# A selective scan on four engines: one activation table set, a bank of its own for the in-projection, GpSimd's states moved, and VectorE's two products as one instruction

## The reference

```
xc = conv1d(x, conv_w) + conv_b                     # 4 taps, one channel at a time
x_dbl = xc @ xproj_w.T                              # 64 dt columns, 16 B, 16 C
dt = clip(x_dbl[:64] @ dtproj_w.T + dtproj_b, 1e-5, 1.0)
u = clip(xc, -10, 10)
delta = softplus(dt + dtproj_b)
A = -exp(A_log)
h[n](t) = exp(delta(t) * A[n]) * h[n](t-1) + delta(t) * u(t) * B[n](t)      # n = 0..15
y(t) = sum_n h[n](t) * C[n](t) + u(t) * D
```

## Time and profile before

| | us |
|---|---|
| median of 3 runs | 9635.69 (9633.86 to 9641.92) |
| the profiled execution | 9635.57 |
| its span | 9633.7 |
| busy: PE, DVE, ACT, POOL | 7457.1, 7666.2, 5757.0, 7469.2 |
| TensorE's mean granted clock | 0.869 of full speed |

### The profile page before, as it was taken

The page is one execution under the profiler, slowest core; times in us unless marked ns, Lnnn a source line. Parts: engine busy times, 40 slices in busy tenths (PEclk is TensorE's granted clock), DMA queues, the critical chain, the costliest instruction groups (busy, mean ns, idle before and its releaser), DMA issues. The chain is left out here.

```text
span 9633.7 us, 148574 instructions
## 1 busy us (share of the span) xinstructions
PE 7457.1 (77%) x28632; PEld 4225.4 (44%) x28632; DVE 7666.2 (80%) x8365; ACT 5757.0 (60%) x12996; POOL 7469.2 (78%) x3329
## 2 busy tenths in 40 slices
PE   7477778787878787865587777787777778659999
PEld 3243444444444444444244444444444444434444
DVE  7924989898989898999298989898989898964444
ACT  3634767676767676766376767676767676640000
POOL 2115999999999999999299999999999999961110
PEclk9689998888888888876788989898989898869999
DMA  2263121212121212110223232323232322133442
GB/s 80 60 184 113 59 100 58 100 57 100 57 100 58 99 58 100 57 62 20 96 67 108 68 108 67 108 64 108 66 106 70 106 68 101 46 126 132 139 140 82
DMA packets 638321, 842.03 MB, mean 87 GB/s; under 512 B 210320, under 2 KB 357776, under 8 KB 620688
## 3 DMA queue, kind: packets, MB, share of 16 engines
q1 hardware_dynamic: 638096, 839.98, 26.9%
HBM read 586.47 MB, written 253.28 MB: 87 GB/s over the span
## 5 line engine op out<-in xcount | busy, mean ns | idle before, releaser
L1102 POOL TENSOR_TENSOR fwd_w<-fwd_du,fwd_bcast_b 128x2048 f32<-128x2048 f32 x504 | 2275.4, 4527 | 19.4 <-DMA fwd_bcast_b<-bc 3.5
L1102 POOL TENSOR_TENSOR bwd_w<-bwd_du,bwd_bcast_b 128x2048 f32<-128x2048 f32 x504 | 2275.8, 4528 | 15.9
L1174 DVE TENSOR_TENSOR_SCAN bwd_h<-bwd_da,bwd_state,bwd_w 128x512 f32<-128x512 f32 x1536 | 1879.0, 1269 | 2.0 <-POOL bwd_w L1102 2.0
L1174 DVE TENSOR_TENSOR_SCAN fwd_h<-fwd_da,fwd_state,fwd_w 128x512 f32<-128x512 f32 x1536 | 1878.9, 1269 | 2.0 <-POOL fwd_w L1102 2.0
L909 PE MATMUL bwd_yT<-all_ident,bwd_hc 128*128 128x128 f32 x6144 | 1058.8, 306 | 899.4 <-DVE bwd_hc L1186 895.8
L909 PE MATMUL fwd_yT<-all_ident,fwd_hc 128*128 128x128 f32 x6144 | 1036.9, 301 | 827.5 <-DVE fwd_hc L1186 823.7
L1023 ACT ACTIVATE fwd_da<-fwd_delta,fwd_aneg 128x512 f32<-128x512 f32 x2048 | 1399.5, 686 | 148.2 <-DVE fwd_h L1174 146.6
L1023 ACT ACTIVATE bwd_da<-bwd_delta,bwd_aneg 128x512 f32<-128x512 f32 x2048 | 1399.2, 686 | 148.0 <-DVE bwd_h L1174 146.5
L909 PEld LDWEIGHTS bwd_yT<-all_ident,bwd_hc 128*128 128x128 f32 x6144 | 785.1, 155 | 1455.9 <-DVE bwd_hc L1186 1181.8
L909 PEld LDWEIGHTS fwd_yT<-all_ident,fwd_hc 128*128 128x128 f32 x6144 | 773.1, 153 | 1394.8 <-DVE fwd_hc L1186 1096.1
L1186 DVE TENSOR_TENSOR fwd_hc<-fwd_h,fwd_bcast_c 128x512 f32<-128x512 f32 x1536 | 1005.2, 681 | 369.0 <-ACT fwd_state L992 338.7
(11 more groups left out here) (181 smaller groups left out, 11538.7 us busy)
## 6 DMA issues: line engine op xcount, KB each, us to landing
bwd_win<-winx SPq DMA_DIRECT2D x128, 512.0 KB, 3.3
fwd_win<-winz SPq DMA_DIRECT2D x128, 512.0 KB, 3.5
yT<-bwd_y_out SPq DMA_DIRECT2D x129, 256.0 KB, 2.7
yT<-fwd_y_out SPq DMA_DIRECT2D x129, 256.0 KB, 3.2
fwd_x<-x_pad SPq DMA_DIRECT2D x128, 257.5 KB, 2.7
n_xin<-x SPq DMA_DIRECT2D x64, 512.0 KB, 4.2
x_pad<-bwd_x SPq DMA_DIRECT2D x128, 256.0 KB, 2.9
xc<-bwd_xc_out SPq DMA_DIRECT2D x128, 256.0 KB, 2.0
```

Source lines behind the costliest of these rows:

```text
L1102: nc.gpsimd.tensor_tensor(w[:, g], du[:, s].unsqueeze(1).to_broadcast([P, G, T]), bcast_b[:, g * G:(g + 1) * G], ALU.mult).then_inc(S["w_d ...
L1174: nc.vector.tensor_tensor_scan(flip(h_slot(n)), flip(da[:, p % 3]), flip(w[:, n // G, n % G]), state_at(j, s, end, n), ALU.mult, ALU.add). ...
```

## The change

Four things change, all inside `stage_scan`:

1. `preload_act_table_set("natural_log_exp_and_others")` stands once per direction, in the prologue. The built program then has no table load in the loops.
2. da has two banks in place of three; `misc` is split in two, `dt_ps` (dt and the convolution) and `in_ps` (the in-projection). ScalarE saves h[n-2] ahead of exp n, and waits for scan n-2.
3. GpSimd's states are 2, 5, 8 and 11, so that VectorE's are 0, 1, 3, 4, 6, 7, 9, 10 and 12 to 15: each pair is followed by a scan of one of GpSimd's states, but for the last two pairs. The steps at which the other pieces stand move with it. On GpSimd the clip of dt is written as min, then max.
4. VectorE multiplies both states of a pair in one instruction of 128x1024 (`weigh_two`), over both banks of h and two neighbouring slots of hc.

```diff
-PN = [0, 3, 6, 9]
+PN = [2, 5, 8, 11]
...
-        da = sc.ps("da", [P, 3, T])
+        da = sc.ps("da", [P, 2, T])
...
-        misc = sc.ps("misc", [P, T])
+        dt_ps, in_ps = sc.ps("dt_ps", [P, T]), sc.ps("in_ps", [P, T])
...
-        LATE = 5
-        IN, IN2, CONV, PROJ, SKIP = 2, 7, 8, 13, 12
-        POOL_AT = [5, 9, 10, 14]
+        LATE = 3
+        IN_AT, IN2_AT, CONV, PROJ, SKIP = (0, 2), (8, 11), 5, 11, 11
+        POOL_AT = [5, 8, 11, 14]
...
                     for n in range(NS):
-                        act.wait_ge(S["scan_done"], m * 32 + (s * 16 + n - 2 + SCR))
+                        act.wait_ge(S["scan_done"], m * 32 + (s * 16 + n - 1 + SCR))
+                        save(j, s, end, n)
...
-                        nc.scalar.activation(da[:, (s * NS + n) % 3], delta[:, s], ACT.Exp,
+                        nc.scalar.activation(da[:, n % 2], delta[:, s], ACT.Exp,
                                              scale=aneg[:, s, n:n + 1]).then_inc(S["exp_done"], 1)
...
+                nc.scalar.preload_act_table_set("natural_log_exp_and_others")
...
-                nc.gpsimd.tensor_scalar(v[:], dt[:], 1e-5, 1.0, ALU.max, ALU.min).then_inc(S["v_done"], 1)
+                nc.gpsimd.tensor_scalar(v[:], dt[:], 1.0, 1e-5, ALU.min, ALU.max).then_inc(S["v_done"], 1)
...
                     weigh_c(ub, 0, k)
                     weigh_b(s, ub, 3, k)
-                    weigh_c(ub, 1, k)
-                    weigh_c(ub, 2, k)
                     if late:
                         clip_v(ub + 1)
-                        weigh_c(ub, 3, k)
+                    weigh_c(ub, 1, k)
+                    if late or not nxt:
+                        weigh_c(ub, 2, k)
                     if nxt:
                         scan_input(1 - s, ub + 1, p_loads)
+                        if not late:
+                            weigh_c(ub, 2, k)
                         weigh_b(1 - s, ub + 1, 0, k2, single=late)
-                    if not late:
-                        weigh_c(ub, 3, k)
+                    weigh_c(ub, 3, k)
...
+                    def weigh_two(n):
+                        p, i = s * NS + n + 1, s * NV + VN.index(n) + 1
+                        for g in sorted({n // G, (n + 1) // G}):
+                            dve.wait_ge(c_loaded[g], k * LOAD + LOAD)
+                        dve.wait_ge(S["scan_done"], m * 32 + p + 1 + SCR)
+                        dve.wait_ge(S["hc_used"], m * (2 * NV) + i + 1)
+                        if a or not end or s == 0 or n + 1 < NS - 2:
+                            dve.wait_ge(S["h_saved"], m * (2 * NS) + (p + 3))
+                        nc.vector.tensor_tensor(hc[:, (i - 1) % NOUT:(i - 1) % NOUT + 2], h[:],
+                                                bcast_c[:, n:n + 2], ALU.mult).then_inc(S["hc_done"], 2)
 
                     for n in range(NS):
                         scan(n)
-                        if n in VN and VN.index(n) % 2:
-                            weigh(VN[VN.index(n) - 1])
-                            weigh(n)
+                        if n in PN:
+                            weigh_two(n - 2)
+                        if n in (NS - 3, NS - 1):
+                            weigh_two(n - 1)
```

More of the change, by code:

```diff
@@ L856, in pair @@
                     for n in range(NS):
[L857 to L865, removed]
-                            dt_matmul(1 - s, (m + s) * (NPL * LOAD) + NPL * LOAD)
-                            if late:
-                                open_projection()
[L869 to L886, removed]
-                            projection(1, ma)
-                            close_projection()
-                        if n == SKIP:
-                            pe.wait_ge(S["ud_done"], ub + 3)
-                            for tb in range(TB):
-                                nc.tensor.matmul(yT[:, tb], ud[:, s, tb * P:(tb + 1) * P], ident[:],
-                                                 is_transpose=True, start=False, stop=False)
                         if n in POOL_AT:
@@ L1028, in pair @@
+                        if with_in and not (end and s == 1) and n == 7:
+                            in_copy(s, ma, m)
+                        if nxt and n == ln_at:
+                            ln_step(b_p1)
+                        if n == ud_at:
                             nc.scalar.activation(ud[:, s], u[:, s], ACT.Copy,
                                                  scale=skip[:, s]).then_inc(S["ud_done"], 1)
-                        if nxt and n == read_at:
-                            act.wait_ge(p_in[1 - s], (m + s) * (NPL * LOAD) + NPL * LOAD)
-                            dt_read(1 - s, m * 2 + s + 2)
@@ L1033, in pair @@
-                        if nxt and n in ln_steps:
-                            softplus_tail(1 - s, m * 2 + s + 2, ln_steps.index(n))
-                        if a and n == 5 and not late:
-                            diagonal(s, ma)
-                        if a and end and s == 0 and n == 12:
+                        if a and not late and n == 10:
+                            xc_copy(s, ma)
+                        if a and end and s == 0 and n == 13:
                             diagonal(1, ma)
-                        if with_in and not (end and s == 1) and n == 9:
-                            in_copy(s, ma, m)
@@ L1041, in pair @@
-                        if with_in and end and s == 0 and n == 14:
+                        if with_in and end and s == 0 and n == 15:
                             in_copy(1, ma, m)
-                        if a and not end and n == 14:
-                            xc_copy(s, ma)
-                        if late and n == 2:
-                            xc_copy(0, ma)
+                        if late and n == 4:
+                            xc_copy(1, ma)
                         if late and n == 5:
-                            xc_copy(1, ma)
@@ L1049, in pair @@
-                        if late and n == 7:
                             proj_copy(k + 1)
@@ L1056, in between @@
                 dt_read(0, 1)
-                for step in range(3):
-                    softplus_tail(0, 1, step)
-                nc.scalar.preload_act_table_set("exp_and_others")
+                abs_step(0, 1)
+                exp_step(0, 1)
+                ln_step(1)
+                relu_step(0, 1)
             def prologue():
```

121 lines of the change are left out of this document (79 added, 42 removed).

## The result

| | us |
|---|---|
| before, median of 4 runs | 9634.78 (9631.48 to 9641.92) |
| after, median of 4 runs | 9911.96 (9908.77 to 9922.27) |
| ratio | 1.0289, 95% interval [1.0271, 1.0306] |
| predicted | 9239 (9145 to 9430) |

The account below looks back on a forecast made before the run. VectorE (27.34 us a block) and GpSimd (27.17) nearly level, taken as 27.5 with coupling, against 29.05 before: gain 1.55 x 256 = 397 us, 9635.6 - 397 = 9239 us, range 9145 to 9430.

Parts of the forecast that it names:

- TensorE at nothing: TensorE's in-projection gets its own bank, starts at the block's first step, has until 10.2 us: cost nothing.
- The wait behind a fused product: On VectorE the next scan starts 0.04 us behind the product's end, so a pair occupies 1.25, six 7.50.
- The two waits for copies: VectorE's products of (12,13) and (14,15) wait for ScalarE's copied last column: 0.48 us each, 0.96 per block.
- The rule that a semaphore costs nothing extra: Skill's rule on VectorE, not adopted: six pairs would take 6.7 us, VectorE's need would be 0.8 lower.
- VectorE's sum: VectorE's need per block: scans 18.88, fused pairs 7.50, waits for copies 0.96, together 27.34 us.
- rival (b): ScalarE's lead too short in a few places: up to 1 us more on VectorE, 9418 us; chance 0.13.
- Handover with two da banks: ScalarE's exp is ready 0.98 us after the scan's end, VectorE at 1.09: fits with 0.11 to spare.
- rival (c): Scan-to-exp handover with two banks longer than laid together, at ten places per block: slower, 10,110 us; chance 0.05.
- GpSimd: GpSimd's clip of dt falls from 1.917 to 0.615 us, its need per block from 28.47 to 27.17.
- rival (d): Pairs' wait free and copies hidden on VectorE, so GpSimd's 27.17 us is the floor: 9154 us; chance 0.10.
- Rival (a): GpSimd's clip of dt keeps its 1.92 us, so GpSimd needs 28.47 per block: 9520 us; chance 0.10.
- ScalarE's tables: Both ScalarE table loads leave the loop, 2.56 us per block; worth nothing by itself, lets state copies come in time.

Follow-up runs that it names:

- with two products: The changed kernel with each fused pair of products as two separate instructions, nothing else undone: 9137.99 us, 0.9485 of the kernel before.
- by load: The changed kernel with the in-projection in the loops cut to 4 of its 8 products, result incomplete: 9525.67 us, 0.9893 of the kernel before.
- by place: The changed kernel with ScalarE's copy of the in-projection at step 9 instead of 7, convolution and its followers later: 9582.81 us, 0.9945 of before.
- by clock: The changed kernel, still fused, with seven added products of zeros on TensorE in blocks without a chunk's end: 9471.52 us, 0.9834 of before.

## Why the prediction was wrong

- **TensorE at nothing: the step that failed.** The prediction says of the in-projection "It has until 10.2 us for eight matmuls" and "Its cost is nothing", and gives no duration for them. It ended at 13.15. At the full clock and with two products this chain (transposes, dt, in-projection) ends at 9.8, only 0.4 us inside the slot, so two things that the prediction didn't ask for decide: when the chain starts and at which clock it runs. The fused product hands over 0.37 us later, and the longer gaps go with a granted clock of 0.50 just there, which costs 3.0 us of TensorE's time. In the block shown ScalarE's copy then waits 2.57 us and VectorE's scan 8 waits 2.12. Removing it by load (386 us), by place (329) or by clock (440) gives 1.3 to 1.7 us a block; the run by clock leaves the kernel's own work and order as they are.
- **What the trace before could have told.** The low clock was there already: 0.50 from 1562 to 1565, and the first four records of the in-projection took 3.37 us, where four later in the same block took 1.88. ScalarE's copy had little slack too; it waited 40.0 us for TensorE backward.

```profile
1561.84 1.12 PE L909 MATMUL bwd_yT<-all_ident,bwd_hc 128*128 128x128 f32 x4 [2.02 <-DVE bwd_hc L1186]
1562.75 3.37 PE L807 MATMUL bwd_misc<-bwd_hn,bwd_win 128*128 128x512 f32 x4
```

- **The wait behind a fused product.** Taken as 0.04 from the earlier trace rows; it is 0.14, and the product and scan hold VectorE 1.34 to 1.39 us, not 1.25. Six came to 8.14 us in the block shown, not 7.50. The [0.15] at the other row was the nearer one. That fusing is a loss on VectorE was foreseen (0.36 + 0.96 us, of which 0.17 would show beyond GpSimd's 27.17); with the clock held up 334 us show, about 1.3 a block beyond GpSimd's cycle.
- **The two waits for copies.** Forecast 0.48 each, found 0.52 each (2.89 against 2.37), of which 0.43 shows as idle time. Right.
- **The rule that a semaphore costs nothing extra** (the Trainium skill, "VectorE: DVE Perf Modes", "The DRAIN you can't avoid") would have given 6.7 us for the six pairs. Measured 8.14: the trace disagrees more than the prediction said. That independent scans overlap is no part of the disagreement, for the section itself says that an instruction which isn't held starts earlier.
- **VectorE's sum.** The block shown is 30.67: 2.12 of stall, and 28.55 where 27.34 was forecast. The 1.21 between are 0.64 at the products, 0.10 at the copies, and 0.47 at the four stretches of three scans (14.63 without the stall, 14.16 forecast). Of this 0.21 is in the second stretch: ScalarE's copy of state 4 stood behind two steps of the softplus and came late (1571.05), as rival (b) had it, and the product started at 1571.34.
- **Handover with two da banks, rival (c).** Its mechanism didn't come: from the first of two scans to the start of the third it takes 2.41 us (1562.64 to 1565.05 in the trace) against 2.36 before, where (c) needed 0.17 more at each of ten places to undo the gain. The slower side came by a chain that no rival named.
- **GpSimd.** The clip takes 0.61 us. Its cycle with two products is 27.1 (from one clip of dt at 1578.77 to the next at 1605.85, neither waiting), forecast 27.17, and rival (d), GpSimd's floor at 9154, is what the kernel without the fusing measured (9138). Rival (a) was priced at 281 us and measured 299. In the changed kernel GpSimd waits for dt, 491.6 us backward, where under 0.4 a block was forecast.
- **ScalarE's tables.** No load is left in the loops. Right.

For the other three parts the working holds: by its own figures they alone would reach GpSimd's floor, 256 x (29.05 - 27.17) = 481 us, and they measured 497. It failed on the fourth.

## What to carry to other kernels

Merging two instructions leaves one fewer, but hands the first result over later; ask of each engine behind it what it does in the longer gap. For TensorE that question has two parts, when it starts and at which clock, and here the second cost more (3.0 us against 0.37). Where the last engine of a chain is at its limit in the trace before (ScalarE's copy already waited for TensorE there, 40.0 us backward), a term of "nothing" needs its own sum. And before fusing, see whether the first half hides a wait for the second: here it hid a copy of 0.5 us, twice a block.

## What was not expected of the hardware

- TensorE's clock fell to 0.50 in the middle of a busy loop, and its work there took nearly twice as long (1.97 for 1.04, 2.07 for 1.12). The length of the last gap doesn't tell when: it was full behind 2.93 us and 0.50 behind 2.73 in one kernel, and at the low level behind 0.58 in another. The kernels with and without fusing differ little in the mean clock (0.87 and 0.89), but in what the slow stretch falls on. Seven useless products a block made the kernel 4.4% faster.
- On GpSimd the same clip took 1.91 us as max, min and 0.61 as min, max.
- A VectorE clip of 0.42 us took up to 3.9 beside GpSimd's long products.
